# Channel attention in a decoder: the turned scores one head at a time, the turn of the maxima last in its step, two small DVE operations moved, and three unit-matrix products per half

## The chip, the cores and the metric

The kernel runs on one NeuronCore of a Trainium2 chip. The metric is the device time of one execution in microseconds. Five engines work side by side, each through its own instructions in order, and meet at semaphores: PE (TensorE, matmuls), DVE (VectorE), ACT (ScalarE), POOL (GpSimd) and SP (SyncE), which here issues the DMAs.

## The reference

Two decoder layers over 32 x 64 tokens of width 256. The change lies in the second layer's cross attention, which attends between channels. It reads x (normalised) and the context as 16 tiles of 128 tokens; a tile is cut into 32 heads of 4 rows, and a head's 256 columns attend to each other:

```python
def _L1_xattn_ref(qkv, y):
    bs, width, length = qkv.shape
    ch = width // N_HEADS                      # 4 rows of a head
    q = qkv.reshape(bs * N_HEADS, ch, length)
    k = v = y.reshape(bs * N_HEADS, ch, -1)
    scale = 1.0 / math.sqrt(math.sqrt(ch))
    weight = jnp.einsum('bct,bcs->bts', q * scale, k * scale)
    weight = jax.nn.softmax(weight.astype(jnp.float32), axis=-1)
    a = jnp.einsum('bts,bcs->bct', weight, v)
    return a.reshape(bs, -1, length)
```

Ahead of it come attention, cross attention, a feed-forward layer and an attention with linear biases; behind it comes a mixture of 32 experts.

## The kernel before

The stage is software-pipelined by hand. One **slot** t is four heads (one in each group of 32 array rows, `CH_RGS` = 4); a tile has eight slots (`CH_SETS`), a **half** has four (`CH_HALF`), so there are 128 slots and 32 halves. Each slot takes two **steps** n = 2t and 2t+1 (`pair` 0 and 1), of two heads each. In step n, `tensor_step` does for PE, in this order:

1. scores of slot t, two heads, into one of two pairs of PSUM banks (`A`). They wait until DVE has read the bank pair two users before (`s_maxed`).
2. between them, the *turned* scores (keys on the partitions) of an older slot b, 13 steps back, two heads, into three banks (`T`) used in rotation. Both heads wait together for the exponential that frees the later bank (`s_exped`).
3. every eighth step (pair 0, t a multiple of 4; here called the **turn step**): the maxima `m` of the finished half are turned by one transpose into the bank that would be next.
4. the mixing with the values of a slot 16 steps back (L1603). At the first slot of a half it waits for the copy of the last half's outputs (`s_okept`).

DVE (`vector_step`) does one maximum over 128x1024 scores in each step (`top`, L1637), which is what the two score banks are read for. In the turn step it then writes the negated maxima from PSUM to `mT` (L1661), from where SP sends them to the query rows that the turned scores read. `top` of the step after a turn step uses the same bank pair as `top` of the turn step itself, since the transpose has taken the pair between them. ACT takes exp of each turned head (L1623, 128x512) and copies each half's outputs from PSUM (L1632).

A tile's outputs then go round by DRAM, in SP's queue (`sync`), with index n for the tile whose middle is being worked on:

```python
            if 0 <= n - 2 < TILES:
                load_total(n - 2)        # L1490, waits for the stored outputs
            ...
            if 2 * n < CH_HALVES:
                load_max(2 * n)          # L1479, waits for mT of half 2n
            stage(2 * n)                 # L197, a weight chunk of the experts
            ...store_out(2 * n - 2)      # L1483, then queries L1468
                store_inverse(n - 2)     # L1494, waits for invert
            ...
                load_out(n - 2)          # L1500, L1501, waits for that store
```

DVE's `invert(n-2)` (L1644) makes the reciprocal of the sums between L1490 and L1494. POOL's `finish(n-2)` (L1728, L1730) waits for `load_out`, multiplies and adds to x; after it POOL sets the values of the next half (L1723), and SP's `load_v` (L1473) and the next `store_out` (L1483) wait for that. DVE's `measured(n-2)` (L238, statistics of the finished tile, used by the experts' stage much later) waits for `finish(n-2)`.

In the kernel before, DVE does `invert` at t mod 8 = 5 and `measured` at t mod 8 = 3, both behind a `top` of pair 1. The turn steps lie at t mod 8 = 4 (middle of a tile) and t mod 8 = 0 (its end).

Of the kernel before, what the change touches and what calls it, by code (L numbers as in the profile page):

```python
# [15 lines left out]
P = 128  # L16
B, S, D = 32, 64, 256
# [235 lines left out]
def normalise(core, dve, out, tile):  # L253

    return core.nc.vector.tensor_scalar(out, core.x[:, tile, :], core.meanvar[:, tile, 0:1], core.rstd[:, tile, :],  # L255
                                        ALU.subtract, ALU.mult)

# [1137 lines left out]
CH_KEYS_AHEAD = 2  # L1395
CH_AHEAD, CH_SETTLE = 4, 12
# [20 lines left out]
def channel_stage(core, keys, moe, jobs=(), first=0):  # L1417
# [39 lines left out]
    def bank(user):  # L1457
        return A[user % 2]
# [3 lines left out]
    def load_q(sp, tile, parts):  # L1462
        sp.wait_ge(s_lo, tile + 1)
        if tile >= CH_RING:
            sp.wait_ge(s_scoredT, 2 * CH_SETS * (tile - CH_RING + 1))
        for n in parts:
            p, ch = n // CH_CH, n % CH_CH
            sp.dma_start(qp[n:P:32, tile % CH_RING], xs[ch:P:CH_CH, tile % 2, p % 2]).then_inc(q_in[tile % 2], 16)  # L1468
# [6 lines left out]
    def sync(sp):  # L1475
# [33 lines left out]
        for n in range(TILES + 3):  # L1509
# [9 lines left out]
            if CH_KEYS_AHEAD <= n + 2 < TILES:  # L1519
                sp.wait_ge(s_scoredT, 2 * CH_SETS * max(0, n + 2 - CH_RING + 1))  # L1520
                sp.wait_ge(k_in[n % 2], 16 * CH_RGS * (n // 2 + 1))
                keys.load(sp, n + 2, k_in[n % 2])
# [28 lines left out]
    def scores_turned(t, pair, u):  # L1551
        tile, set8 = t // CH_SETS, t % CH_SETS
        for g in (2 * pair, 2 * pair + 1):
            rows = slice(32 * g, 32 * (g + 1))
            last = nc.tensor.matmul(ps[:, T[(t * CH_RGS + g) % len(T)], u * D:(u + 1) * D], kp[rows, tile % CH_RING, set8, u * P:(u + 1) * P],  # L1555
                                    qp[rows, tile % CH_RING, set8, :], start=True, stop=True)
        return last

    def tensor_step(pe, n):
        t, pair = n // 2, n % 2  # L1560
        tile = t // CH_SETS
        b, b_pair = (n - CH_B_LAG) // 2, (n - CH_B_LAG) % 2
        if t < CH_SLOTS:
            if n % (2 * CH_SETS) == 0:
                pe.wait_ge(q_in[tile % 2], 16 * CH_KEYROWS * (tile // 2 + 1))
                pe.wait_ge(k_in[tile % 2], 16 * CH_RGS * (tile // 2 + 1))
            user = (a_first, a_second)[pair](t)
            if user >= 2:
                pe.wait_ge(s_maxed, user - 1)
        if 0 <= b < CH_SLOTS:  # L1570
# [5 lines left out]
            done = b * CH_RGS + 2 * b_pair + 2 - len(T)  # L1576
            if done > 0:
                pe.wait_ge(s_exped, done)
        for u in range(KD):
# [4 lines left out]
            if 0 <= b < CH_SLOTS:  # L1584
                last = scores_turned(b, b_pair, u)
                if u == KD - 1:
                    last.then_inc(s_scoredT, 1)
        if pair == 0 and t % CH_HALF == 0 and 0 < t <= CH_SLOTS:
            half = t // CH_HALF - 1
            user = a_turn(half)  # L1590
            pe.wait_ge(s_maxed, max(user - 1, a_second(t - 1) + 1))
            nc.tensor.transpose(ps[0:32, bank(user), 0:P], m[:, half % 2].rearrange("p g s u -> p (g s u)"), core.ident).then_inc(s_scored, 1)
        c, u = (n - CH_C_LAG) // 2, (n - CH_C_LAG) % 2
        if 0 <= c < CH_SLOTS:
            half, j = c // CH_HALF, c % CH_HALF
            if u == 0:
# [4 lines left out]
                pe.wait_ge(s_exped, CH_RGS * (c + 1))  # L1601
            for g in range(CH_RGS):
# [3 lines left out]
            if u == KD - 1:  # L1606
                last.then_inc(s_mixed, 1)

# [6 lines left out]
    def scalar(act):  # L1615
        for b in range(CH_SLOTS + CH_HALF):
            for g in range(CH_RGS):
                if b < CH_SLOTS:
                    act.wait_ge(s_scoredT, 2 * b + g // 2 + 1)
# [30 lines left out]
    def vector_step(dve, n):  # L1650
# [11 lines left out]
        if pair == 1 and t % CH_SETS == 5 and tile >= 2:  # L1662
            invert(dve, tile - 2)
        if pair == 1 and t % CH_SETS == 3 and tile >= 3:
            measured(dve, tile - 3)
# [942 lines left out]
```

## Time and profile before

| | |
|---|---|
| median of 3 runs | 1909.52 us (1908.63 to 1910.26) |
| the profiled execution | 1909.29 us, span 1907.5 us |
| mean granted TensorE clock | 0.975 |
| PE, DVE, ACT, POOL busy | 89%, 78%, 54%, 38% of the span |
| the channel stage's own steps | 1138.8 to 1502 us |

The span runs from the first to the last instruction; busy shares are averages over six very different stages, so the stretch of the channel stage is looked at by itself. In rows of a timeline the columns are start, duration, engine, line, operation, what it writes and reads, how many were merged, and in brackets how long the engine sat idle before and what ended that.

### The profile page before, as it was taken

The numbers are of one execution on the slowest core, as the hardware profiler recorded it, in microseconds if no ns is written. First come the engines' busy times: TensorE is split into PE (matmuls) and PEld (weight loads), VectorE is DVE, ScalarE is ACT, GpSimd is POOL, SyncE is SP. The second block draws the span as 40 slices with busy tenths as digits, with TensorE's granted clock in tenths as the row PEclk, the third lists the DMA queues.
The fourth block names the chain that finished last, engine by engine and source line by source line (L and its number), as shares of the span: only waits on it lengthen the run. The fifth ranks groups of instructions, "written<-read, shape, count | busy, mean of one in ns | idle before, by whom it ended". The sixth has DMA issues, their size and how long they took to land.

```text
span 1907.5 us, 43444 instructions
## 1 busy us (share of the span) xinstructions
PE 1704.7 (89%) x15840; PEld 1002.3 (53%) x15840; DVE 1488.9 (78%) x2884; ACT 1031.4 (54%) x2056; POOL 720.2 (38%) x965
## 2 busy tenths in 40 slices
PE   5999999789999999979977996777777889999998
PEld 2665666456777777755544541222222356656555
DVE  5776666689989899858887889999999478676654
ACT  2666565345555555534336765888888533323222
POOL 4635321287777677612345452444531000000000
PEclk9999999999999999989989997999999999999999
DMA  9601010000000000000001211333321022222121
GB/s 254 177 24 51 29 42 2 6 18 21 13 13 15 9 9 7 2 9 1 1 1 39 60 36 52 94 90 96 97 74 42 17 79 95 86 65 70 63 84 50
DMA packets 87663, 94.92 MB, mean 50 GB/s; under 512 B 17569, under 2 KB 63265, under 8 KB 87457
## 3 DMA queue, kind: packets, MB, share of 16 engines
q1 hardware_dynamic: 83712, 87.76, 16.1%
q10 hardware_dynamic: 2976, 2.32, 0.5%
q8 instruction: 128, 2.10, 0.5%
q0 software_dynamic: 768, 2.10, 0.4%
q14 instruction: 79, 0.64, 0.1%
HBM read 78.51 MB, written 10.22 MB: 47 GB/s over the span
## 4 chain that ended last, share of the span: by engine, by line
PE 23%; DVE 22%; issue 6%; POOL 3%; ACT 2%; DMA 0%; DVEq 0%; POOLq 0%; ACTq 0%
PE ps L286 18%; DVE arena L1637 14%; POOL arena L1192 2%; PE ps L1904 1%; PE ps L1547 1%; PE ps L1901 1%; DVE arena L2485 1%; DVE arena L2481 0%; DVE arena L1246 0%; DVE arena L255 0%; POOL arena L2058 0%; DVE arena L2416 0%; DVE arena L2414 0%; DVE arena L1997 0%; ACT arena L2357 0%
## 5 line engine op out<-in xcount | busy, mean ns | idle before, releaser
L286 PE MATMUL ps<-arena 128*128 128x512 f16 (+6 forms) x6464 | 1087.7, 323 | 53.1 <-POOL arena L1192 11.1
L286 PEld LDWEIGHTS ps<-arena 128*128 128x128 f16 (+1 forms) x6464 | 600.9, 99 | 438.1 <-issue 36.7
L1623 ACT ACTIVATE arena<-ps 128x512 f32<-128x512 f32 x512 | 278.6, 598 | 73.1 <-PE ps L1555 50.8
L1637 DVE TENSOR_REDUCE arena<-ps 128x4 f32<-128x1024 f32 x256 | 305.6, 1218 | 11.7 <-PE ps L1547 11.4
L1547 PE MATMUL ps<-arena 31*128 31x256 f16 x1024 | 102.5, 277 | 72.9 <-ACT arena L1623 51.7
L1603 PE MATMUL ps<-arena 128*32 128x256 f32 x2048 | 164.9, 394 | 2.8 <-ACT arena L1632 0.6
L2475 DVE TENSOR_TENSOR arena<-ps,arena 128x512 f32<-128x512 f32 x96 | 66.1, 688 | 124.4 <-ACT arena L2367 109.2
L2367 ACT ACTIVATE arena<-ps 128x512 f32<-128x512 f32 x96 | 57.1, 596 | 175.5 <-PE ps L286 175.0
L1547 PEld LDWEIGHTS ps<-arena 31*128 31x128 f16 x1024 | 34.7, 92 | 188.5 <-DVE arena L1637 150.3
L1096 POOL TENSOR_TENSOR arena<-arena 128x512 f32<-128x512 f32 x96 | 98.8, 1043 | 46.1 <-DVE arena L232 44.7
L669 POOL TENSOR_TENSOR arena<-arena 128x256 f32<-128x256 f32 x64 | 39.4, 615 | 194.6 <-DVE arena L635 194.6
L519 ACT ACTIVATE arena<-ps,arena 128x512 f32<-128x512 f32 x64 | 44.0, 688 | 114.9 <-PE ps L286 114.9
L1555 PE MATMUL ps<-arena 32*128 32x256 f16 x1024 | 101.4, 276 | 0.9 <-ACT arena L1623 0.2
L2357 ACT ACTIVATE arena<-arena 128x512 f16<-128x512 f32 x96 | 60.1, 626 | 73.7 <-DVE arena L2481 73.3
L1192 POOL TENSOR_TENSOR arena<-arena 128x512 f16<-128x512 f32 x32 | 50.3, 1575 | 113.8 <-ACT arena L1349 110.5
L208 POOL TENSOR_TENSOR arena<-arena 128x256 f16<-128x256 f32 (+5 forms) x72 | 86.2, 1197 | 5.8
L1110 POOL TENSOR_TENSOR arena<-arena 128x256 f32<-128x256 f32 x80 | 58.2, 728 | 70.2 <-DVE arena L1021 70.1
L955 ACT ACTIVATE arena<-ps 128x512 f16<-128x512 f32 x64 | 38.2, 597 | 83.0 <-PE ps L881 83.0
L206 POOL CAST arena<-arena 128x256 f16<-128x256 f32 (+5 forms) x72 | 45.2, 628 | 95.3 <-DMA arena<-in_L_ffn_gate_up_proj 67.7
L1101 POOL TENSOR_TENSOR arena<-arena 128x512 f32<-128x512 f32 x64 | 67.1, 1049 | 25.3 <-DVE arena L1056 25.2
L1020 DVE TENSOR_TENSOR arena<-ps,arena 128x512 f32<-128x512 f32 x80 | 54.9, 686 | 27.4 <-ACT arena L950 21.7
L588 DVE TENSOR_TENSOR arena<-ps,arena 128x512 f16<-128x512 f32 x64 | 43.9, 686 | 40.7 <-ACT arena L508 40.7
(203 smaller groups left out, 2928.5 us busy)
## 6 DMA issues: line engine op xcount, KB each, us to landing
arena<-moe_cw SPq DMA_DIRECT2D x64, 192.0 KB, 2.8
arena<-moe_cw SPq DMA_DIRECT2D x64, 128.0 KB, 2.8
arena<-in_L_ffn_gate_up_proj SPq DMA_DIRECT2D x16, 384.0 KB, 3.4
ch_out<-arena SPq DMA_DIRECT2D x32, 128.0 KB
arena<-moe_cw SPq DMA_DIRECT2D x64, 64.0 KB, 2.7
ch_keys<-arena SPq DMA_DIRECT2D x48, 64.0 KB, 2.0
arena<-ch_keys SPq DMA_DIRECT2D x64, 48.0 KB
arena<-arena SPq DMA_DIRECT2D x192, 16.0 KB
```

The costliest lines, as they stand in the source:

```text
L208: nc.gpsimd.tensor_tensor(lo, raw, hi, ALU.subtract).then_inc(core.s_split, 1)
L286: last = nc.tensor.matmul(out, a, b, start=start and n == 0, stop=stop and n == len(pairs) - 1, skip_group_check=not group)
L1096: nc.gpsimd.tensor_tensor(a4, a4, spread(rms[:, s % 2, u * CROSS_KVH:(u + 1) * CROSS_KVH], CROSS_HD), ALU.mult).then_inc(scaled.sem, 1)
L1101: nc.gpsimd.tensor_tensor(prob[:, k % 2], e[:, k % 2], spread(inv[:, k % 2, :], CROSS_KEYS), ALU.mult).then_inc(probs.sem, 1)
L1192: nc.gpsimd.tensor_tensor(hT[1][:, k % FFN_MEMBERS], h[:, k // FFN_MEMBERS % 2, k % FFN_MEMBERS], hT[0][:, k % FFN_MEMBERS], ALU.subtract) ...
L1547: last = nc.tensor.matmul(ps[:, bank(user) + n, u * D:(u + 1) * D], qp[rows, tile % CH_RING, set8, u * P:(u + 1) * P], kp[rows, tile % CH_ ...
L1555: last = nc.tensor.matmul(ps[:, T[(t * CH_RGS + g) % len(T)], u * D:(u + 1) * D], kp[rows, tile % CH_RING, set8, u * P:(u + 1) * P], qp[ro ...
L1603: last = nc.tensor.matmul(ps[32 * g:32 * (g + 1), O, 0:D], vz[:, half % 2, u, g, j, :], pT[:, c % 3, g, u, :], start=j == 0 and u == 0, st ...
L1623: nc.scalar.activation(pT[:, b % 3, g], ps[:, T[n % len(T)], :].rearrange("p (u t) -> p u t", u=KD), ACT.Exp, scale=CH_SCALE).then_inc(s_e ...
L1637: nc.vector.tensor_reduce(m[:, half % 2, 2 * half_pair:2 * half_pair + 2, j, :], ps[:, bank(user):bank(user) + 2, :].rearrange("p g (u s) ...
L2357: nc.scalar.activation(hT[0][:, b % 4, :], h[b % MOE_HELD], ACT.Copy).then_inc(s_hi, 1)
L2475: nc.vector.tensor_tensor(h[n % MOE_HELD], ps[:, U[n % 2], :], silu[:, n % 2, :], ALU.mult).then_inc(s_gated, 1)
```

## The change

- The turned scores' two heads are no longer issued together: the first is interleaved with the scores and waits for its own bank, the second follows behind them with a wait of its own. `s_scoredT` counts heads instead of pairs, and the waits on it are scaled.
- In the turn step the transpose of the maxima is issued after the mixing, last.
- `keep_warm` puts three products of the unit matrix with itself (fp32, 128x128 by 128) into the unused columns of the outputs' bank, ahead of the mixing of each half's first slot. By the step numbers this is in the turn step, behind the wait for the copy of the outputs.
- DVE does `invert(n-2)` at t mod 8 = 4 and `measured(n-2)` at the next t mod 8 = 0, each directly behind the write of `mT` in the turn step, instead of three steps later and seven steps later.

```diff
+def keep_warm(nc, out, operand, times):
+    for _ in range(times):
+        nc.tensor.matmul(out, operand, operand, start=True, stop=True, skip_group_check=True)
...
+CH_WARM = 3
...
+        def bank_free(g):
+            done = b * CH_RGS + g + 1 - len(T)
+            if done > 0:
+                pe.wait_ge(s_exped, done)
...
-            done = b * CH_RGS + 2 * b_pair + 2 - len(T)
-            if done > 0:
-                pe.wait_ge(s_exped, done)
+            bank_free(2 * b_pair)
         for u in range(KD):
...
             if 0 <= b < CH_SLOTS:
-                last = scores_turned(b, b_pair, u)
+                last = scores_turned(b, 2 * b_pair, u)
                 if u == KD - 1:
                     last.then_inc(s_scoredT, 1)
-        if pair == 0 and t % CH_HALF == 0 and 0 < t <= CH_SLOTS:
-            (transpose of the maxima)
+        if 0 <= b < CH_SLOTS:
+            bank_free(2 * b_pair + 1)
+            for u in range(KD):
+                last = scores_turned(b, 2 * b_pair + 1, u)
+            last.then_inc(s_scoredT, 1)
...
                 pe.wait_ge(s_exped, CH_RGS * (c + 1))
+                if j == 0:
+                    keep_warm(nc, ps[:, O, D:D + P], core.ident, CH_WARM)
             (mixing)
+        if pair == 0 and t % CH_HALF == 0 and 0 < t <= CH_SLOTS:
+            (transpose of the maxima)
...
-                    act.wait_ge(s_scoredT, 2 * b + g // 2 + 1)
+                    act.wait_ge(s_scoredT, CH_RGS * b + g + 1)
...
             nc.vector.tensor_scalar(mT[:, half % 2], ...).then_inc(s_maxed, 1)
-        if pair == 1 and t % CH_SETS == 5 and tile >= 2:
-            invert(dve, tile - 2)
-        if pair == 1 and t % CH_SETS == 3 and tile >= 3:
-            measured(dve, tile - 3)
+            if t % CH_SETS == CH_HALF and tile >= 2:
+                invert(dve, tile - 2)
+            if t % CH_SETS == 0 and 3 <= tile < TILES:
+                measured(dve, tile - 3)
```

Lines in round brackets stand for code that is moved or kept as it is.

## Rows read from the trace of the kernel before

**Rows 1.** Page: the chain that ended last, share of the span by line.
```profile
PE ps L286 18%; DVE arena L1637 14%; POOL arena L1192 2%; PE ps L1904 1%; PE ps L1547 1%; PE ps L1901 1%; DVE arena L2485 1%; DVE arena L2481 0%; DVE arena L1246 0%; DVE arena L255 0%; POOL arena L2058 0%; DVE arena L2416 0%; DVE arena L2414 0%; DVE arena L1997 0%; ACT arena L2357 0%
```

**Rows 2.** Windows; busy PE, PEld, DVE, ACT, POOL, granted clock, DMA share, GB/s.
```profile
1137.00:1172.00 35.00, 19.09 (x214) 6.41 (x211) 31.52 (x57) 10.53 (x22) 11.06 (x20) 0.61 0.14 39
1197.00:1477.00 280.00, 218.37 (x3483) 68.36 (x3483) 271.02 (x271) 238.84 (x460) 111.58 (x212) 1.00 0.30 81
```

**Rows 3.** Waits, 1157 to 1477: total us, times, longest; the last of SP's queue.
```profile
POOL arena L1728 <- DMA arena<-ch_inverse: 73.1, 13, 12.8
PE ps L1547 <- DMA arena<-arena: 2.0, 4, 1.3
...
SPq L1473 <- POOL arena L1723: 36.9, 12, 3.7
```

**Rows 4.** Timeline of DVE over a half and the next one's start.
```profile
1292.19 0.27 DVE L1661 TENSOR_SCALAR arena<-ps 32x128 f16<-32x128 f32 x1
1292.76 8.51 DVE L1637 TENSOR_REDUCE arena<-ps 128x4 f32<-128x1024 f32 x7 [0.31 <-PE ps L1547]
1301.19 0.42 DVE L238 BATCH_NORM_STATS2 arena<-arena 128x6 f32<-128x256 f32 x1
...
1302.65 0.27 DVE L1661 TENSOR_SCALAR arena<-ps 32x128 f16<-32x128 f32 x1
...
1303.22 3.65 DVE L1637 TENSOR_REDUCE arena<-ps 128x4 f32<-128x1024 f32 x3 [0.31 <-PE ps L1547]
1306.79 0.54 DVE L1644 RECIPROCAL arena<-arena 128x64 f32<-128x64 f32 x1
1307.25 5.69 DVE L1637 TENSOR_REDUCE arena<-ps 128x4 f32<-128x1024 f32 x5
1312.86 0.27 DVE L1661 TENSOR_SCALAR arena<-ps 32x128 f16<-32x128 f32 x1
```

**Rows 5.** Timeline of DVE: the same write of mT ten tiles apart.
```profile
1219.60 0.27 DVE L1661 TENSOR_SCALAR arena<-ps 32x128 f16<-32x128 f32 x1
...
1427.69 0.27 DVE L1661 TENSOR_SCALAR arena<-ps 32x128 f16<-32x128 f32 x1
```

**Rows 6.** Timeline of POOL: the ends of two tiles' finish.
```profile
1295.99 0.73 POOL L1730 TENSOR_TENSOR arena<-arena 128x256 f32<-128x256 f32 x1
...
1316.38 0.73 POOL L1730 TENSOR_TENSOR arena<-arena 128x256 f32<-128x256 f32 x1
1337.18 0.73 POOL L1730 TENSOR_TENSOR arena<-arena 128x256 f32<-128x256 f32 x1
```

**Rows 7.** Timeline of SP's queue from one middle L1479 to the next.
```profile
1305.44 0.56 SPq L1479 DMA_DIRECT2D arena<-arena  x1
1309.46 0.45 SPq L1494 DMA_DIRECT2D ch_inverse<-arena  x1
1311.85 0.63 SPq L1500 DMA_DIRECT2D arena<-ch_out  x1
1317.73 0.39 SPq L1473 DMA_DIRECT2D arena<-in_ctxT  x1
1322.17 0.62 SPq L1490 DMA_DIRECT2D arena<-ch_out  x1
...
1325.84 0.56 SPq L1479 DMA_DIRECT2D arena<-arena  x1
```

**Rows 8.** Timelines of ACT and PE in one turn step, and of PE later.
```profile
1301.06 0.39 ACT L1632 ACTIVATE arena<-ps 128x256 f32<-128x256 f32 x1
...
1301.33 0.28 PE L1592 MATMUL ps<-arena 128*32 128x128 f32 x1
1301.71 0.64 PE L1603 MATMUL ps<-arena 128*32 128x256 f32 x8
...
1518.14 1.05 PE L2272 MATMUL ps<-arena 128*128 128x128 f32 x8
```

**Rows 9.** Timeline of DVE in the low-clock stretch: one maximum and the wait before it.
```profile
1169.69 1.22 DVE L1637 TENSOR_REDUCE arena<-ps 128x4 f32<-128x1024 f32 x1 [0.33 <-PE ps L1547]
```

More of the change, by code:

```diff
@@ L1464, in load_q @@
         if tile >= CH_RING:
-            sp.wait_ge(s_scoredT, 2 * CH_SETS * (tile - CH_RING + 1))
+            sp.wait_ge(s_scoredT, CH_RGS * CH_SETS * (tile - CH_RING + 1))
         for n in parts:
@@ L1519, in sync @@
             if CH_KEYS_AHEAD <= n + 2 < TILES:
-                sp.wait_ge(s_scoredT, 2 * CH_SETS * max(0, n + 2 - CH_RING + 1))
+                sp.wait_ge(s_scoredT, CH_RGS * CH_SETS * max(0, n + 2 - CH_RING + 1))
                 sp.wait_ge(k_in[n % 2], 16 * CH_RGS * (n // 2 + 1))
@@ L1549, in scores, with scores_turned @@
         return last
-    def scores_turned(t, pair, u):
+    def scores_turned(t, g, u):
         tile, set8 = t // CH_SETS, t % CH_SETS
[L1553 to L1557, printed above, removed]
+        rows = slice(32 * g, 32 * (g + 1))
+        return nc.tensor.matmul(ps[:, T[(t * CH_RGS + g) % len(T)], u * D:(u + 1) * D], kp[rows, tile % CH_RING, set8, u * P:(u + 1) * P],
+                                qp[rows, tile % CH_RING, set8, :], start=True, stop=True)
     def tensor_step(pe, n):
@@ L1584, in tensor_step @@
             if 0 <= b < CH_SLOTS:
-                last = scores_turned(b, b_pair, u)
+                last = scores_turned(b, 2 * b_pair, u)
                 if u == KD - 1:
                     last.then_inc(s_scoredT, 1)
-        if pair == 0 and t % CH_HALF == 0 and 0 < t <= CH_SLOTS:
[L1589 to L1592, printed above, removed]
+        if 0 <= b < CH_SLOTS:
[3 more added lines that the diff above has]
+            last.then_inc(s_scoredT, 1)
         c, u = (n - CH_C_LAG) // 2, (n - CH_C_LAG) % 2
@@ L1607, in tensor_step @@
                 last.then_inc(s_mixed, 1)
+        if pair == 0 and t % CH_HALF == 0 and 0 < t <= CH_SLOTS:
+            half = t // CH_HALF - 1
+            user = a_turn(half)
+            pe.wait_ge(s_maxed, max(user - 1, a_second(t - 1) + 1))
+            nc.tensor.transpose(ps[0:32, bank(user), 0:P], m[:, half % 2].rearrange("p g s u -> p (g s u)"), core.ident).then_inc(s_scored, 1)
     def tensor(pe):
```

## The prediction, as recorded before the changed kernel was run

> **What bounds the kernel now.** I read the chain that ended last first [rows 1]. After the matmuls of the other stages, DVE's maximum L1637 is its largest piece, 14% of the span: the channel stage is where the change acts and where DVE sets the pace. The windows give the stage by itself [rows 2]. From 1197 to 1477 us DVE is busy 271.0 of 280 us, ACT 238.8, PE 218.4, and the granted clock is 1.00, the 2.4 GHz level; only up to 1172 us is it lower (0.61). So the stage has a DVE pace of a step, and 9 us of DVE idle to be had there at most.
>
> The timeline of DVE shows the pace inside a half [rows 4]. Two kinds of half alternate. From the mT write at 1292.19 to that at 1302.65 is 10.46 us, from there to 1312.86 is 10.21, so a tile takes 20.67. Seven maxima from 1292.76 take 8.51 us of gapless record, (8.51 - 1.22) / 6 = 1.213 each; five behind the reciprocal, when DVE is behind and its input is ready, take 5.69, (5.69 - 1.22) / 4 = 1.12 each. DVE is thus not quite at its own pace even where it looks full: 0.09 us of each PE-paced step is lost, and the records hide it, since a maximum that overlaps the next one shows no gap. After each turn there is 0.31 us of real idle.
>
> The third thing to see is outside these engines. The waits [rows 3] have POOL waiting for ch_inverse 13 times, 73.1 us, SP for POOL's L1723 12 times, 36.9 us, and PE for an SBUF-to-SBUF DMA 4 times. A tile's outputs go round through SP, the DMAs and POOL, and this round has a period of its own: SP's L1479 comes at 1305.44 and again at 1325.84, 20.40 us later [rows 7], and in this tile it waits for neither PE nor DVE (L1661 was done at 1302.92, the wait before L1473 is POOL's). Ten tiles, from the mT write at 1219.60 to that at 1427.69, average 20.81 us [rows 5], more than the 20.67 of an undisturbed tile: the round already holds PE up now and then. The two periods lie so close that what is saved on one of them alone is mostly lost on the other.
>
> **The moved operations on DVE.** `invert` and `measured` cost 0.46 us (1306.79 to the next maximum at 1307.25) and 0.33 (L238 and the maximum behind it) wherever they stand. Behind mT they lie in the 0.31 us of idle, so placing them there could give back some 0.3 us each. But they also wait. `invert(n-2)` waits for L1490's landing. Its latest place in the old timeline would be mT's end, 1302.92; L1490 is issued 3.67 us before L1479 (1322.17 and 1325.84 [rows 7]), so at 1301.77 here, and the landing is not in a row. Bounds: at once, or by the next issue that needs such a landing, 2.39 us (L1494 at 1309.46 to L1500 at 1311.85). I take 2.3, so 1304.1, a wait of 1.2 us at the old timing.
>
> `measured(n-2)` is the serious one. It moves from 1301.19 to behind the mT write of 1292.19. It waits for `finish`, whose last operation starts at 1295.99 and ends at 1296.72 [rows 6]. Before, that left 4.5 us of slack; in the new place it is 4.26 us *late*. What is queued behind it on DVE is the `top` of the step after the turn; PE waits for that two steps later, and ACT for PE. Added: 1296.72 + 0.05 + 0.33 = 1297.10 instead of 1292.76 for the next maximum, 4.34 us once.
>
> **Why this is not paid only once.** `finish` hangs on the tile's middle mT write by SP's order: L1479 waits for mT, and L1494, L1500, then `finish` stand behind it in the queue. From L1479 to the end of `finish` is 1305.44 to 1317.11 = 11.67 us, and in the next tile 1325.84 to 1337.91 = 12.07 [rows 6, 7]; I take 11.85. With DVE now held up for `finish` at the tile's end, there is a closed loop:
> mT written, to L1479: 0.03; to the end of `finish`: 11.85; to the next maximum: 0.05 + 0.33; from there to the next middle mT write: x.
>
> x follows from the half [rows 4, 8]. Floor by DVE: seven maxima at 1.12 to 1.13, an eighth of 1.22, mT 0.27 less overlap 0.08: 9.33. The chain through PE: the split wait lets the scores start when the maximum two steps back ends, so PE runs ahead of DVE by about a step instead of 0.4 us, and the steps shrink to 1.13. Before, ACT's output copy ended at 1301.45, 8.69 us after the maximum at 1292.76; with seven steps 0.085 shorter and some 0.5 more lead, 7.6. Then 0.26 to the first product, the warm products, the mixing 0.45 (its 0.64 less the tail that a next matmul overlaps), transpose and semaphore 0.32, mT 0.27. A warm product is priced by L2272: eight records of the same shape, two to a product, in 1.05 us, (1.05 - 0.28) / 7 = 0.11 each, so 0.22 a product and 0.66 for three. Sum: 7.6 + 0.26 + 0.66 + 0.45 + 0.32 + 0.27 = 9.56; I take 9.6. If ACT's copy stays at its old 8.69, x is 10.65: both ends are kept.
>
> Period of the loop: 0.03 + 11.85 + 0.38 + 9.6 = 21.86 us, against 20.81 measured: +1.05 per tile. The DVE and PE loop alone would be 9.6 + 9.6 + 0.3 + 0.46, about 19.9, and SP's round 20.4; neither is the largest now. The wait for L1490's landing then hides: L1490 runs ahead of mT by more in the longer period.
>
> **Sum.** Full lag first appears at the turn near 1230: +4.3. From there nine tiles to near 1431 run in the loop: 9 x 1.05 = +9.4. In the last two to three tiles no queries are loaded and the queue is shorter, so DVE and PE go at their own 19.9 against 20.67: -1.5. Behind the stage's last maxima one group of warm products stands in PE's chain: +0.66, less about 0.2 for the split wait. Total +12.7, on the profiled 1909.29: 1922.0. The median of the runs shown is 0.23 above it, so 1922.
>
> **The clock.** The low stretch ends at 1172 and the first warm products come at about 1166; from 1197 to 1477 the clock is full [rows 2], so they have nothing to raise and are counted as 0.66 us each. The Trainium skill (TensorE: Matmul & The Clock Gate, Part 1) says that activity releases the throttle and idleness brings it back. By it the products would be worth something only if PE's idle time grew, which it does here, some 2 us per tile; that is a rival below.
>
> The Trainium skill (DMA: Bandwidth & Descriptors, "Two cost components") puts about 2.0 us on a DMA as fixed cost. From L1500's issue to `finish` the rows have 1315.6 (0.73 before 1316.38) less 1311.85, 3.7 us, for two transfers issued together; by the page's figure the loop would be some 1.7 us shorter and fall below SP's round. The time would then be that of the second rival below. The rows disagree with it here and decide.
>
> **Rivals.**
> *Faster: the waits are satisfied in time.* If `finish` ended before the end-of-tile mT write, DVE would go at 1.13 a step with its extras in the gap, and the stage would gain what SP's round allows at least and 20.67 - 19.9 = 0.77 x 13 tiles = 10 at most: 1899. It needs `finish` 4.3 us earlier than it ends before [rows 6], and nothing in the diff moves it forward. In the loop above it decides from the point where L1479 to the end of `finish` is under 10.8 us, which brings the period back to 20.81. Chance 0.07.
> *No change: SP's round swallows all.* If only that round counts, the time stays at 1906 to 1912. It is against the semaphore count, which makes DVE wait. Chance 0.06.
> *Warm products and late transpose at full price.* x = 10.65, ACT's copy no earlier: +2.1 per tile, 4.3 + 18.9 - 0.5 = +23, 1932. Against it: the exponentials have room. Chance 0.13.
> *The clock falls in the new gaps.* In the low stretch a step took 1.22 + 0.33 = 1.55 us [rows 9] against 1.213. If two to four steps per tile ran so, 0.7 to 1.4 us per tile, 10 to 17 us more: about 1936. Chance 0.04.
> The forecast has 0.70.
>
> **Range.** The loop's bounds are x from 9.33 to 10.65 and L1479 to `finish` from 11.3 (0.4 under the shorter tile) to 12.07: from 4.3 + 9 x 0.23 - 1 = +5 to the +23 above. Of the forecast's own cases I leave the lowest out: 1913 to 1934. The forecast's own range is 1914 to 1930. Changes of under 0.2%, 3.8 us, can hardly be told from none. Faster 0.07, same 0.07 (the second rival and the forecast's lowest end), slower 0.86.
>
> **What the profile after would show.** L238 directly behind L1661 at the tile's end, with idle before it released by POOL L1730, 1.5 to 2 us in each tile from the fourth on; the same mT write 21.9 us apart; maxima 1.13 apart, not 1.213; SP's L1479 in mid-tile waiting for L1661; PE busy 21 us more (96 products of 0.22). I am wrong if DVE never waits for POOL, if the period stays at 20.8 or below, or if the granted clock leaves 1.00 in the stage.

## The result, and the profile after

The changed kernel takes 1930.34 us (median of 4, 1928.29 to 1932.6), the kernel before 1909.89 (median of 4, 1908.63 to 1912.96): a ratio of 1.0104, interval 1.009 to 1.0117. It is slower, as predicted, and by 20.4 us where 12.7 were forecast; 1930.34 lies just above the forecast's own range (1914 to 1930) and inside the stated one (1913 to 1934). The profiled execution took 1929.33 us, its span 1927.5 (before: 1909.29 and 1907.5).

Lines have moved: the maximum is now L1653 (before L1637), the write of mT L1677 (L1661), the reciprocal L1660 (L1644), the turned scores L1561, the mixing L1614 (L1603), the transpose L1623 (L1592), ACT's exponential L1639, its output copy L1648 (L1632), POOL's setting of the values L1739 (L1723), `finish` L1744 and L1746 (L1728, L1730); in SP's queue `load_q` L1475, `load_v` L1480, `load_max` L1486 (L1479), `load_total` L1497 (L1490), `store_inverse` L1501 (L1494), `load_out` L1507 and L1508 (L1500, L1501). The products are L262, `measured` is L238 in both.

The page's chain that ended last, which answers to [rows 1]:

```profile
PE ps L292 18%; DVE arena L1653 5%; PE ps L1614 2%; SPq L1475 2%; DMA arena<-ch_inverse 2%; POOL arena L1198 2%; DMA ch_inverse<-arena 1%; PE ps L1920 1%; PE ps L1554 1%; PE ps L262 1%; PE ps L1917 1%; ACT arena L1639 1%; DVE arena L2501 1%; DVE arena L2497 0%; DMA ch_out<-arena 0%
```

DVE's maximum had 14% of it and has 5%. In its place stand SP's query issues, the store of the inverses, their load, the mixing and the products. The chain now runs through SP, the DMAs to and from DRAM, PE, ACT and DVE. The waits of the stage, 1197 to 1477 us (total, times, longest), and those of SP's queue from 1240 on:

```profile
DVE arena L238 <- POOL arena L1746: 20.3, 12, 2.1
DVE arena L1677 <- PE ps L1623: 15.0, 25, 1.0
PE ps L262 <- ACT arena L1648: 7.1, 18, 0.6
...
SPq L1486 <- DVE arena L1677: 53.0, 22, 6.1
```

The first row is the predicted one: `measured` waits for POOL's last operation in each tile, 1.7 us on the mean. The last is the loop's other joint: SP's `load_max` waits for mT.

The timeline of DVE over the half behind the new wait, and two writes of mT ten tiles apart (answers to [rows 4, 5]):

```profile
1240.78 0.28 DVE L1677 TENSOR_SCALAR arena<-ps 32x128 f16<-32x128 f32 x1 [0.87 <-PE ps L1623]
...
1295.87 0.28 DVE L1677 TENSOR_SCALAR arena<-ps 32x128 f16<-32x128 f32 x1 [0.47 <-PE ps L1623]
1297.36 0.43 DVE L238 BATCH_NORM_STATS2 arena<-arena 128x6 f32<-128x256 f32 x1 [1.21 <-POOL arena L1746]
1297.70 9.13 DVE L1653 TENSOR_REDUCE arena<-ps 128x4 f32<-128x1024 f32 x8
1307.30 0.28 DVE L1677 TENSOR_SCALAR arena<-ps 32x128 f16<-32x128 f32 x1 [0.47 <-PE ps L1623]
1307.51 0.53 DVE L1660 RECIPROCAL arena<-arena 128x64 f32<-128x64 f32 x1
...
1330.14 0.28 DVE L1677 TENSOR_SCALAR arena<-ps 32x128 f16<-32x128 f32 x1 [0.77 <-PE ps L1623]
...
1465.88 0.28 DVE L1677 TENSOR_SCALAR arena<-ps 32x128 f16<-32x128 f32 x1 [0.87 <-PE ps L1623]
```

L238 stands right behind L1677 with idle released by POOL. Eight maxima take 9.13 us, (9.13 - 1.22) / 7 = 1.13 each: DVE works at its own pace again, and waits 0.47 us for the transpose at the half's end. The period is (1465.88 - 1240.78) / 10 = 22.51 us, against 20.81 [rows 5].

The other stations of the loop: POOL (answers to [rows 6]),

```profile
1296.48 0.73 POOL L1746 TENSOR_TENSOR arena<-arena 128x256 f32<-128x256 f32 x1
...
1318.71 0.73 POOL L1746 TENSOR_TENSOR arena<-arena 128x256 f32<-128x256 f32 x1
```

SP's queue (answers to [rows 7]),

```profile
1307.61 0.56 SPq L1486 DMA_DIRECT2D arena<-arena  x1
...
1311.63 0.44 SPq L1501 DMA_DIRECT2D ch_inverse<-arena  x1
1314.23 0.63 SPq L1507 DMA_DIRECT2D arena<-ch_out  x1
```

and ACT and PE in the turn step between (answers to [rows 8]):

```profile
1304.92 0.39 ACT L1648 ACTIVATE arena<-ps 128x256 f32<-128x256 f32 x1
...
1305.57 0.91 PE L262 MATMUL ps<-arena 128*128 128x128 f32 x6 [0.55 <-ACT arena L1648]
1306.41 0.64 PE L1614 MATMUL ps<-arena 128*32 128x256 f32 x8
1306.98 0.28 PE L1623 MATMUL ps<-arena 128*32 128x128 f32 x1
```

From `load_max` at 1307.61 to the end of `finish` at 1319.44 is 11.83 us; POOL's end at 1297.21 to L238 is 0.15, L238 to the maximum 0.34, and from the maximum at 1297.70 to mT's end at 1307.58 is 9.88.

One thing is in the trace that the forecast did not have. The windows (columns as in [rows 2]):

```profile
1197.00:1477.00 280.00, 234.00 (x3355) 83.64 (x3349) 242.93 (x250) 216.51 (x423) 110.35 (x204) 0.95 0.28 79
1320.00:1321.50 1.50, 0.31 (x8) 0.13 (x8) 1.50 (x3) 0.00 (x0) 1.43 (x3) 1.00 0.65 232
1321.50:1325.00 3.50, 3.50 (x40) 0.90 (x40) 3.27 (x4) 2.38 (x5) 3.29 (x4) 0.51 0.49 126
```

The stage's granted clock is 0.95, not 1.00. Behind the wait for `finish` PE is idle, then it is granted 0.51, the 1.2 GHz level, for 3.5 us. PE's timeline shows the edge:

```profile
1318.83 0.64 PE L1614 MATMUL ps<-arena 128*32 128x256 f32 x8
1321.19 0.28 PE L1554 MATMUL ps<-arena 31*128 31x256 f16 x2 [1.73 <-DVE arena L1653]
...
1321.53 1.08 PE L1614 MATMUL ps<-arena 128*32 128x256 f32 x8
```

The same eight mixing matmuls take 0.64 us ahead of the gap and 1.08 behind it. Such a stretch begins 6 times between 1240 and 1477, and never there in the kernel before. In the tile with this one the half behind the wait took 10.5 us, from the maximum at 1319.92 to mT's end at 1330.42, instead of 9.88. The six such halves took 10.49 to 10.69 us, 0.74 more than 9.88 on the mean; the four others of the ten tiles took 9.88 each. Every tile has an idle time of PE behind the wait: 1.47 to 1.98 us in the six, 0.89 to 1.53 in the four.

Where the 20 us are: the first write of mT was at 1152.9 before and is at 1148.5, the last at 1478.5 and 1496.4, so the stage itself is 22.3 us longer; behind the last one lie 429.0 and 431.1 us, +2.1; and the stage starts 4.5 earlier, which is no gain of the change (that start lies between 1148.5 and 1155.5 in the profiles of this study, whose kernels have the same code ahead of it).

### The profile page after: what moved, and what is told of

The parts are those of the page before. It is cut to its first block, busy times and chain, and to the rows that moved or that the text cites. A ratio compares the mean times of both kernels' runs of the same rounds, so it can differ in the third digit from the quotient of the medians.

```text
span 1927.5 us, 43766 instructions
## 1 busy us (share of the span) xinstructions
PE 1738.4 (90%) x15971; PEld 1029.6 (53%) x16032; DVE 1482.3 (77%) x2884; ACT 1026.2 (53%) x2056; POOL 720.5 (37%) x965
## 3 DMA queue, kind: packets, MB, share of 16 engines
q8 instruction: 129, 2.11, 0.5%
## 4 chain that ended last, share of the span: by engine, by line
PE 26%; DVE 13%; issue 6%; POOL 4%; DMA 3%; SPq 3%; ACT 2%; DVEq 0%; POOLq 0%; ACTq 0%
PE ps L292 18%; DVE arena L1653 5%; PE ps L1614 2%; SPq L1475 2%; DMA arena<-ch_inverse 2%; POOL arena L1198 2%; DMA ch_inverse<-arena 1%; PE ps L1920 1%; PE ps L1554 1%; PE ps L262 1%; PE ps L1917 1%; ACT arena L1639 1%; DVE arena L2501 1%; DVE arena L2497 0%; DMA ch_out<-arena 0%
## 5 line engine op out<-in xcount | busy, mean ns | idle before, releaser
L1639 ACT ACTIVATE arena<-ps 128x512 f32<-128x512 f32 x512 | 272.4, 599 | 101.4 <-PE ps L1561 98.0
L1653 DVE TENSOR_REDUCE arena<-ps 128x4 f32<-128x1024 f32 x256 | 292.6, 1206 | 2.5 <-PE ps L1554 1.8
L1614 PE MATMUL ps<-arena 128*32 128x256 f32 x2048 | 171.3, 408 | 0.1
L2383 ACT ACTIVATE arena<-ps 128x512 f32<-128x512 f32 x96 | 57.1, 596 | 175.7 <-PE ps L292 175.3
L1554 PE MATMUL ps<-arena 31*128 31x256 f16 x1024 | 105.2, 287 | 48.9 <-DVE arena L1653 46.9
L1561 PE MATMUL ps<-arena 32*128 32x256 f16 x1024 | 117.9, 284 | 0.0
L1554 PEld LDWEIGHTS ps<-arena 31*128 31x128 f16 x1024 | 29.5, 93 | 158.6 <-DVE arena L1653 123.2
```

The source lines that it names most:

```text
L1554: last = nc.tensor.matmul(ps[:, bank(user) + n, u * D:(u + 1) * D], qp[rows, tile % CH_RING, set8, u * P:(u + 1) * P], kp[rows, tile % CH_ ...
L1561: return nc.tensor.matmul(ps[:, T[(t * CH_RGS + g) % len(T)], u * D:(u + 1) * D], kp[rows, tile % CH_RING, set8, u * P:(u + 1) * P], qp[ro ...
L1614: last = nc.tensor.matmul(ps[32 * g:32 * (g + 1), O, 0:D], vz[:, half % 2, u, g, j, :], pT[:, c % 3, g, u, :], start=j == 0 and u == 0, st ...
L1639: nc.scalar.activation(pT[:, b % 3, g], ps[:, T[n % len(T)], :].rearrange("p (u t) -> p u t", u=KD), ACT.Exp, scale=CH_SCALE).then_inc(s_e ...
L1653: nc.vector.tensor_reduce(m[:, half % 2, 2 * half_pair:2 * half_pair + 2, j, :], ps[:, bank(user):bank(user) + 2, :].rearrange("p g (u s) ...
```

## The experiments

Theory A: the moved `measured` closes a loop (DVE waits for POOL's `finish`, which hangs by SP's order on the mT that the same DVE wrote half a tile earlier), and this loop is the loss. Theory B: the loss is PE's part, the products and the late transpose, and the wait only shows it. Theory C: part of the loss is the clock, which falls in the gaps that the wait leaves on PE. A fourth, E, is about what the other parts are worth: SP's round through DRAM has its own period near 20.4 us and takes what they save. The letters are those of the recorded expectations, which add D, F, G and H where they stand.

All readings in one table. The period is over ten tiles, between the starts of two rows of DVE's timeline, L1677 (or L1661), like those above; "low" counts the stretches from 1240 to 1477 us in which the eight mixing matmuls took over 0.9 us, and the clock is that window's granted one.

| kernel | median us | ratio [interval] | profiled us | mT at | period | clock | low |
|---|---|---|---|---|---|---|---|
| before | 1909.89 | | 1909.29 | 1240.26, 1448.35 | 20.81 | 1.00 | 0 |
| changed | 1930.34 | 1.0104 [1.009, 1.0117] | 1929.33 | 1240.78, 1465.88 | 22.51 | 0.96 | 6 |
| e1, moves undone | 1911.77 | 1.001 [0.9999, 1.002] | 1910.29 | 1240.51, 1446.26 | 20.58 | 1.00 | 0 |
| e2, moves alone | 1920.39 | 1.0054 [1.0035, 1.0073] | 1920.69 | 1241.97, 1458.10 | 21.61 | 0.99 | 2 |
| e3, no products | 1919.69 | 1.005 [1.0034, 1.0067] | 1919.66 | 1241.88, 1459.85 | 21.80 | 0.94 | 8 |
| e4, PE's part, no products | 1910.82 | 1.000 [0.9983, 1.0017] | 1910.9 | 1240.83, 1448.19 | 20.74 | 0.99 | 2 |
| e5, `measured` alone | 1932.41 | 1.0109 [1.0095, 1.0124] | 1928.93 | 1244.42, 1465.59 | 22.12 | 0.97 | 4 |
| e6, `invert` alone | 1911.9 | 1.0001 [0.999, 1.0011] | 1916.41 | 1243.65, 1454.51 | 21.09 | 1.00 | 0 |
| e7, e4 + shorter round | 1907.82 | 0.9968 [0.9953, 0.9983] | 1911.42 | 1241.21, 1444.96 | 20.38 | 0.96 | 5 |
| e8, before + shorter round | 1910.08 | 0.999 [0.9979, 1.0001] | 1906.57 | 1238.33, 1444.95 | 20.66 | 1.00 | 0 |
| e9, e1 + shorter round | 1908.75 | 0.9987 [0.9978, 0.9996] | 1910.41 | 1243.92, 1447.21 | 20.33 | 1.00 | 0 |
| e10, e9, products elsewhere | 1923.74 | 1.007 [1.0056, 1.0083] | 1922.66 | 1242.94, 1458.40 | 21.55 | 0.99 | 2 |
| e11, changed, `finish` earlier | 1911.28 | 1.0001 [0.9991, 1.0011] | 1916.06 | 1244.19, 1452.58 | 20.84 | 1.00 | 0 |
| e12, e9, one product | 1902.37 | 0.9964 [0.995, 0.9978] | 1899.86 | 1238.04, 1437.96 | 19.99 | 1.00 | 0 |

Each ratio is against runs of the kernel before beside it; their medians were 1909.18 to 1911.56. Period, clock and low stretches are of the one profiled execution, which can lie off the median: it is the slowest of its runs in e6 and e7 and the fastest in e5, e10 and e12. The mean clock over the whole kernel is known for every run; on the mean of the runs it is 0.968, 0.970 and 0.967 in e3, e4 and e7, which have no products, 0.974 in e1, e9 and e12, which have them in the turn step and not the loop, and 0.974 to 0.976 in the kernel before.

**e1, the DVE moves undone** in the changed kernel (e2 is the opposite edit, on the kernel before):

```diff
-            if t % CH_SETS == CH_HALF and tile >= 2:
-                invert(dve, tile - 2)
-            if t % CH_SETS == 0 and 3 <= tile < TILES:
-                measured(dve, tile - 3)
+        if pair == 1 and t % CH_SETS == 5 and tile >= 2:
+            invert(dve, tile - 2)
+        if pair == 1 and t % CH_SETS == 3 and tile >= 3:
+            measured(dve, tile - 3)
```

> The changed kernel with DVE's two moved operations back in their old places (invert at t mod 8 = 5, measured at t mod 8 = 3, pair 1); the split wait, the late transpose and the three products stay. Theory A (the move of measured closes a loop mT, SP's queue, finish on POOL, DVE, which gives the period): DVE's waits for POOL go, the tile period falls from 22.5 us to SP's round of about 20.4 to 20.8, and the early gain of 4.5 us (turn steps up to 1200 us) stays in part: 1903 to 1909 us. Theory B (the products and the late transpose on PE give the time, the waits only sit beside them): 1925 to 1930, about as the changed kernel. Theory C (part of the +20 is the clock falling in PE's gaps while DVE waits): the granted clock stays 1.00 from 1200 to 1480 us.

1911.77 us: 18.6 of the 20.4 us are gone with all of PE's part still in. Its window, 1240 to 1477:

```profile
1240.00:1477.00 237.00, 210.06 (x3114) 81.42 (x3106) 224.57 (x231) 195.64 (x391) 92.57 (x176) 1.00 0.29 80
```

The clock is 1.00 with the products in and the long waits out. This refutes theory B as the main cause, and it agrees with C's condition (clock 1.00). A's time was a little low: what PE's part was to give did not come (the period is only 0.23 below that of the kernel before).

**e2, the moves alone**, on the kernel before.

> The kernel before with DVE's two operations moved as in the change, nothing else of it. Theory A: the loop closes here too, with the old half of about 9.9 us between the resumed maxima and the next mT write: period 0.03 + 11.8 + 0.4 + 9.9 = 22.1 or more, without the gain of the early turn steps, so 1927 to 1935 us. Theory B: 1905 to 1911, since nothing of PE's work changes. Theory C: low-clock stretches of 3.4 us appear here as well.

1920.39 us, +10.4, so only about half of the loss, below what A expected. DVE's timeline:

```profile
1296.38 0.27 DVE L1661 TENSOR_SCALAR arena<-ps 32x128 f16<-32x128 f32 x1
1298.91 0.43 DVE L238 BATCH_NORM_STATS2 arena<-arena 128x6 f32<-128x256 f32 x1 [2.25 <-POOL arena L1730]
1299.25 9.12 DVE L1637 TENSOR_REDUCE arena<-ps 128x4 f32<-128x1024 f32 x8
1308.29 0.27 DVE L1661 TENSOR_SCALAR arena<-ps 32x128 f16<-32x128 f32 x1
```

Here mT comes without any wait behind eight maxima at DVE's pace: x = 1308.56 - 1299.25 = 9.31. With the prediction's other terms the loop is 0.03 + 11.85 + 0.38 + 9.31 = 21.57; 21.61 was measured. The loop's formula holds, and the prediction's lower bound of x, 9.33, is what the old PE order has. That the two agree within 0.04 is in part luck: measured link by link it is 0.03 + 11.69 + 0.49 + 9.41 = 21.62, where 9.41 is 9.31 and what the two low stretches add.

**e3, no products** (`CH_WARM = 0` in the changed kernel), and **e4**, the same with the moves undone too, so PE's split wait and late transpose alone:

> The changed kernel with no unit-matrix products (CH_WARM = 0), all else as changed. Theory A with the products at full price in the half (0.66 us between ACT's copy and the next mT write): period 0.66 shorter per tile, 9 to 12 tiles, 6 to 8 us: 1922 to 1925 us. Theory B: the turn step is freed of the products, 2 x 0.66 per tile or 20 us less: 1910. Theory C: without the products PE is idle longer, more low-clock stretches than the seven between 1200 and 1480 us, and no gain: 1928 to 1935.

> The changed kernel with DVE's operations back and no products: only the split wait and the late transpose are left. Theory A: as e1, since SP's round of 20.4 to 20.8 us is the limit there and the products are hidden under it: within 2 us of e1, 1903 to 1909. Theory B: 0.66 us per half less than e1 or more, 15 to 20 us below it. Theory C: clock 1.00 or a little lower; if the products were what kept it, low stretches appear here and not in e1.

e3's window and its main wait:

```profile
1240.00:1477.00 237.00, 192.12 (x2839) 59.88 (x2834) 213.61 (x221) 190.89 (x375) 89.25 (x169) 0.94 0.28 78
```

```profile
DVE arena L238 <- POOL arena L1746: 21.1, 10, 2.8
```

Without products 1919.69, lower than the 1922 to 1925 expected; with them 1930.34. So the products cost 10.7 us *inside the loop*, where every tile has them between ACT's copy and mT. With the moves undone, e4 and e1, they cost 1.0 us, no more than the noise: there another round sets the pace. And without them the clock falls more often, 8 stretches instead of 6, so the 10.7 is what is left after whatever they give. The moves cost 1919.69 - 1910.82 = 8.9 us without products and 18.6 with them. So half of the 20.4 us needs both: the loop that the move closes, and the products in it. The time of e3 also speaks against C's expectation for it (no gain); its count of low stretches is as C has it, and low stretches appear in e4 and not in e1. e4 equals before: the late transpose and the split wait alone bring nothing that shows.

**e5 and e6, one move each** on the kernel before; e5's edit:

```diff
+            if t % CH_SETS == 0 and 3 <= tile < TILES:
+                measured(dve, tile - 3)
-        if pair == 1 and t % CH_SETS == 3 and tile >= 3:
-            measured(dve, tile - 3)
```

> The kernel before with measured alone moved behind mT at t mod 8 = 0; invert stays at t mod 8 = 5. Theory A (measured closes the loop): as the kernel with both moved (1920.4, period 21.6 us), since invert's wait is covered there: 1918 to 1923 us. Rival D (invert's wait for the landing of the sums makes the cost): as before, 1908 to 1911.

> The kernel before with invert alone moved behind mT at t mod 8 = 4; measured stays at t mod 8 = 3. Theory A: DVE waits for the landing of the sums, which come 2.3 us after L1490, so each tile's phase against SP's round shifts by about 1.2 us once, then the period stays that of SP's round: 1908 to 1912. Rival D: 1918 to 1923.

`invert` alone costs nothing, 1911.9 (no change). (e6 is the like edit for `invert`.) `measured` alone costs 21.5 us, twice as much as both moves together, which I had not expected. SP's queue in e5:

```profile
1312.60 0.56 SPq L1479 DMA_DIRECT2D arena<-arena  x1
...
1317.02 0.35 SPq L1494 DMA_DIRECT2D ch_inverse<-arena  x1
1317.47 1.67 SPq L1468 DMA_DIRECT2D arena<-arena  x3
1319.25 0.63 SPq L1500 DMA_DIRECT2D arena<-ch_out  x1
```

`store_inverse` comes 4.42 us behind `load_max`, against 4.02 [rows 7]: with `invert` left at t mod 8 = 5 it runs three maxima behind mT (1316.45, mT at 1312.31), so the reciprocal is a link of the loop. In e2 `invert` is done by then. From `load_max` to the end of `finish` is 12.06 us on the mean of ten tiles, 11.69 in e2: 0.37 of the 0.51 by which the periods differ, and four low stretches instead of two make up the rest. That is read from one trace of each and not tested by an edit, and it gives 5 of the 11 us between the medians; the other part is not shown. The seat of the loss is `measured`; `invert` early is a help once that loop exists.

**e7, e8, e9: SP's round shortened.** `load_total`, which waits for stored outputs to land, is moved behind `load_max`, which then no longer stands behind that wait:

```diff
-            if 0 <= n - 2 < TILES:
-                load_total(n - 2)
...
             if 2 * n < CH_HALVES:
                 load_max(2 * n)
+            if 0 <= n - 2 < TILES:
+                load_total(n - 2)
```

e7 is e4 with it, e8 the kernel before with it, e9 is e1 with it (so e7 with the three products).

> The changed kernel without products, with DVE's operations in their old places, and in SP's queue load_total (with its wait for the stored outputs) placed behind the five queries and load_max of the tile's middle instead of ahead of them. Theory E (in the kernel before and without the moves, SP's round of DRAM trips, 20.4 to 20.8 us a tile, sets the period and PE waits for the mT transfer that stands in it): load_max no longer waits for the landing, the PE and DVE pace of about 19.9 to 20.0 us shows: 0.6 to 0.8 us less per tile over 12 tiles, 1900 to 1904 us. Rival F (the stage is DVE's 20.7 anyway): 1910, as e4.

> The kernel before with only that reordering of SP's queue. Theory E: its own PE pace is 20.67 against the 20.81 measured, so only 0.14 x 12 = 1.7 us can come: 1907 to 1909. Rival F: the same as before within 1 us.

> As the run with the shortened round (DVE's operations in their old places, load_total behind load_max), but with the change's three products in the turn step. There the clock fell for 3.4 us about every second tile without them, and an undisturbed tile took 19.98 us, a disturbed one about 1 us more. Theory G (the products keep the clock up and cost less than they bring once nothing else binds): no low-clock stretch between 1240 and 1477 us, every tile 20.3 to 20.5 us (the products' 0.8 us in one half show in part): 0 to 2 us faster or slower than without, 1904 to 1910. Theory H (products only cost): 2 x 0.8 us a tile or some of it, 5 to 10 us slower than without them: 1912 or more.

e8 is no faster beyond doubt: 1910.08, with a period of 20.66 that is the undisturbed pace of a tile in the kernel before (20.67). So PE and DVE bound that kernel together as much as the round does. e4 has the quicker step but the old round, and is no faster either. With both, e7, the period falls to 20.38 and the kernel is 0.3% faster: theory E holds. The traces show the wait that went. In e4 PE stands idle ahead of L1554 six times between 1240 and 1477, 6.1 us in all, for what the profile calls issue; in e7 never. The longest in e4, rows of SP and PE:

```profile
1344.03 0.62 SPq L1497 DMA_DIRECT2D arena<-ch_out  x1
1348.02 0.56 SPq L1486 DMA_DIRECT2D arena<-arena  x1
1349.82 0.28 PE L1554 MATMUL ps<-arena 31*128 31x256 f16 x2 [2.87 <-issue]
```

mT was written at 1342.73, but `load_max` comes behind `load_total` and the queries, and PE goes on 1.8 us after it. (That this idle time is the wait for `load_max` is inferred from the order, the profile does not name it.)

e7 missed the 1900 to 1904 of theory E by some 4 us. DVE's timeline and the window of a low stretch show what held it:

```profile
1301.75 1.22 DVE L1653 TENSOR_REDUCE arena<-ps 128x4 f32<-128x1024 f32 x1 [0.30 <-PE ps L1554]
1303.29 1.23 DVE L1653 TENSOR_REDUCE arena<-ps 128x4 f32<-128x1024 f32 x1 [0.32 <-PE ps L1554]
1304.86 1.23 DVE L1653 TENSOR_REDUCE arena<-ps 128x4 f32<-128x1024 f32 x1 [0.34 <-PE ps L1554]
```

```profile
1301.50:1305.20 3.70, 3.70 (x48) 0.88 (x40) 2.79 (x3) 2.48 (x5) 0.00 (x0) 0.54 0.36 77
```

There a step takes 1.55 us (the 1.55 of [rows 9]), about 1 us lost per stretch, 5 stretches. e9's three products remove them all, but a tile without stretches takes 20.30 to 20.33 instead of 19.98: 1908.75 against e7's 1907.82, no better.

**e10, the products off the turn step**: in e9 the three are moved from ahead of the mixing to the end of the next step, into the free half of the transpose's bank pair.

```diff
-                if j == 0:
-                    keep_warm(nc, ps[:, O, D:D + P], core.ident, CH_WARM)
...
+        if pair == 1 and t % CH_HALF == 0 and 0 < t < CH_SLOTS:
+            keep_warm(nc, ps[:, bank(a_turn(t // CH_HALF - 1)) + 1, 0:P], core.ident, CH_WARM)
```

> As the last one, but the three products stand at the end of the step behind the turn step, into the free half of the bank pair that the transpose took, where PE has about 1 us of lead over DVE, and not between ACT's copy and the transpose. Theory G: the clock stays up and the tile takes its undisturbed 20.0 us: 0.6 to 0.8 us a tile less than the kernel before over 14 tiles, 1899 to 1903 us. Theory H: no difference to the run without products, 1907, or slower.

A miss, 1923.74 where I had expected 1899 to 1903. DVE's timeline behind the turn, and PE's:

```profile
1298.04 1.23 DVE L1653 TENSOR_REDUCE arena<-ps 128x4 f32<-128x1024 f32 x1 [0.30 <-PE ps L1554]
1299.81 6.88 DVE L1653 TENSOR_REDUCE arena<-ps 128x4 f32<-128x1024 f32 x6 [0.55 <-PE ps L1554]
```

```profile
1298.51 0.94 PE L262 MATMUL ps<-arena 128*128 128x128 f32 x6
```

Behind the turn DVE has caught up with PE and waits for its scores; the products lie right ahead of them. The second maximum waits another 0.55 us. The products' place has no idle of PE that they could fill.

**e11, the changed kernel with `finish` earlier.** Nothing on DVE or PE is touched. In SP's queue `store_inverse` goes right behind `load_max`, and `load_out` ahead of the last queries:

```diff
             if 2 * n < CH_HALVES:
                 load_max(2 * n)
+            if 0 <= n - 2 < TILES:
+                store_inverse(n - 2)
...
                 load_q(sp, n + 2, range(5, 9))
+            if 0 <= n - 2 < TILES:
+                load_out(n - 2)
```

(both are taken out of their old places)

> The changed kernel, all of it, with SP's queue cut short between load_max and finish: store_inverse directly behind load_max, load_out behind the next four queries. From L1486's issue to the end of finish that takes away about 2.0 us of 11.8. Theory A (the loop mT, SP, finish, DVE gives the period of 22.5 us): the period falls by as much, to 20.4 to 20.8, and DVE's waits for POOL shrink: 1908 to 1913 us. Theory B (PE's products and late transpose give the period by themselves): 1926 to 1930.

1911.28 us: 19 of the 20.4 us come back by the order of SP's queue alone. Its SP queue and POOL, and the wait:

```profile
1307.24 0.55 SPq L1486 DMA_DIRECT2D arena<-arena  x1
1307.84 0.45 SPq L1501 DMA_DIRECT2D ch_inverse<-arena  x1
...
1311.79 0.62 SPq L1507 DMA_DIRECT2D arena<-ch_out  x1
```

```profile
1316.65 0.73 POOL L1746 TENSOR_TENSOR arena<-arena 128x256 f32<-128x256 f32 x1
```

```profile
DVE arena L238 <- POOL arena L1746: 4.1, 6, 1.5
```

From `load_max` to the end of `finish` is 1317.38 - 1307.24 = 10.14 us instead of 11.83, and the period is 20.84. This is the case that shows theory A: the loop is what costs, since a shorter link in it, which touches nothing else on DVE or PE, gives the time back. The low stretches went with it (0 in the window), though all three products are still in.

**e12, one product instead of three** in e9.

```diff
-CH_WARM = 3
+CH_WARM = 1
```

> The run with the shortened round and products in the turn step, but one product instead of three. With three the tile took 20.30 us and the clock stayed full from 1240 us; with none an undisturbed tile took 19.98 and five low-clock stretches stood between 1240 and 1477 us. Theory G (the products hold the clock, and each costs PE's turn step about 0.25 us of which part shows): either one product holds the clock too and the tile takes about 20.1, 1904 to 1907 us, or it doesn't, low stretches appear as without products and the time is theirs, 1906 to 1910. Theory H (the low stretches have nothing to do with the products): their number is that of three products, about one.

1902.37 us, 0.9964 [0.995, 0.9978], below both kernels and below the 1904 to 1907 expected. Its window, and PE's turn step:

```profile
1240.00:1477.00 237.00, 204.62 (x3065) 71.79 (x3057) 226.57 (x258) 201.97 (x402) 91.62 (x176) 1.00 0.30 80
```

```profile
1296.52 0.46 PE L262 MATMUL ps<-arena 128*128 128x128 f32 x2 [0.54 <-ACT arena L1648]
1296.91 0.64 PE L1614 MATMUL ps<-arena 128*32 128x256 f32 x8
1297.48 0.28 PE L1623 MATMUL ps<-arena 128*32 128x128 f32 x1
```

The clock is 1.00 with no low stretch, and the period is 19.99, the undisturbed tile of e7. One product from 1296.52 to the mixing at 1296.91 is 0.39 us, three are 0.84 (1305.57 to 1306.41): 0.225 for each further one, and 0.17 once beside the first. Against three products (e9, 0.9987 [0.9978, 0.9996]) one is the faster. Against none (e7, 0.9968 [0.9953, 0.9983]) the runs do not tell: the ratios are alike, and the periods of 19.99 and 20.38 come from e12's fastest and e7's slowest run. That the products hold the clock is seen in all runs; that one product saves time over none is not shown.

## Why the prediction was right, and where its sizes were off

**The mechanism: right, and shown.** DVE waits in each tile for POOL, behind the mT write of the tile's end; the wait closes a loop. e1 (wait out, loss out), e2 and e5 (wait in, loss in) and e11 (wait in, link shortened, loss out) leave no other main cause. The point from which the loop decides, `load_max` to the end of `finish` under 10.8 us, agrees with e11: 10.14 and a period of 20.84. But one of the three signs by which the forecast was to be wrong did come: the granted clock left 1.00 in the stage. And 1930.34 is nearer to the 1932 of the rival "warm products and late transpose at full price" than to 1922. That rival is not what happened: it had ACT's copy no earlier and x = 10.65, and the copy came at 7.6 us and x is 9.88 wherever the clock stays up.

**The link through SP and POOL: right.** 11.85 us was taken; 11.83 in the tile shown, 11.67 on the mean of ten. The step from POOL's end to the next maximum was 0.15 + 0.34 instead of 0.38, 0.1 short. The rows decided rightly here against the shorter DMA cost that the recorded text weighed, though its 3.7 us are no measure of one transfer: the second load is issued 0.67 us after the first (L1501 at 1312.52), and each moves 128 KB.

**x, from there to mT: mis-sized.** 9.6 was taken and 9.88 measured. The copy on ACT ended 7.6 us after the resumed maximum (1305.31 - 1297.70), exactly as taken. The products took 0.84 us instead of 0.66, since the price came from a row of eight records in series (0.22 each, e12 confirms 0.225) and left out the 0.17 once beside the first. The mixing ahead of the transpose took 0.57 instead of 0.45. That is the 0.3. e2 and e3 put a size on what the late transpose and the products do to the loop: the period is 21.61 with neither, 21.80 with the transpose late, 22.51 with both. All three hold low stretches; in the tiles without one x is 9.31, 9.32 and 9.88. So the late transpose (with the split wait) costs the loop nothing, and three products cost it 0.56 us a tile of their 0.84.

**The clock: what the forecast left at 0.04 happened beside it.** The recorded text named "the clock falls in the new gaps" as a rival; it is no rival but comes on top. The period by the measured links without it is about 0.03 + 11.67 + 0.49 + 9.88 = 22.07. Six of the ten tiles lost 0.74 us on the mean, 0.44 a tile, which gives 22.51, as measured. So of the excess of 0.65 over the forecast's 21.86, two thirds are the clock, and one third is the turn step's 0.28 and 0.11 behind `finish`, less 0.18 for the shorter link through SP. The price in the rival, 0.7 to 1.4 us per tile, holds for a tile with a stretch at its lower end (0.61 to 0.81), but only six tiles in ten had one.

**The clock again: "they have nothing to raise".** This is wrong for the quicker step. With split wait and late transpose and no products, the clock falls 2, 5 and 8 times (e4, e7, e3), although no gap in e7 comes from the loop. The kernel before, with its slower step, keeps 1.00. There is something to raise, and one product raises it (e12). At the stage's start the granted clock reached 1.00 near 1164.5 in the changed kernel and near 1172 in the one before; but e1, with the products, has 1167.5 and e3, e4 and e7, without them, 1168 to 1172, so no run shows that they raise it there. The Trainium skill (TensorE: Matmul & The Clock Gate, Part 1) has it that idleness brings the throttle back; the changed kernel agrees, where each of the six stretches comes behind 1.47 to 1.98 us of idle on PE. Why the quicker step in e7 is more exposed than the slower one before, which leaves PE idle for longer (busy 16.13 us of 20.60 in a tile, against 16.56 of 19.99 in a tile of e7 without a stretch), no run here settles. The traces give a hint: the idle time of e7 comes in a longer piece. Its longest is 0.78 us, once in each tile behind the turn step, and all five stretches begin right behind it; the kernel before has at most 0.44 there, and e12 and e9, with products, hardly anything over 0.6. It is no more than a hint, since single gaps of 1.26 us before and 1.48 in e1 passed without a fall.

**The sum.** Forecast +4.3 for the first lag, +9.4 for nine tiles, -1.5 at the end, +0.5 behind: 12.7. Measured: +5.0 up to the write of mT at 1240.78, +17.0 over the ten tiles from there (1.70 each instead of 1.05, and one tile more in the loop), +0.3 at the end, where the gain of 1.5 did not come, +2.1 behind the stage. The 5.0 is not one lag of 4.3: DVE waits for `finish` already near 1207, 2.11 us, and again near 1230, 1.95, each time with a low stretch behind it. The stage's earlier start takes 4.5 off. Of the +2.1 I can name only the product group and a clock of 0.95 instead of 0.98 between 1477 and 1580 us; it was not tested.

**What the other parts give.** That DVE and PE alone would run at "about 19.9" was right: e12 has 19.99. That SP's round near 20.4 would swallow it was right as well (e1 and e4 no faster than before), and moving one wait in its queue gave it free (e7, e12). PE's busy time rose by 33.7 us, not 21: the page has 1738.4 against 1704.7. Low-clock stretches count as busy, but they are the smaller part of it: e1, with none between 1240 and 1477, has 1735.3, and e4, without products, 1715.5.

**Still open:** why the clock falls in the quicker pattern; what else makes e5 slower than e2; the 7 us between starts of the stage in kernels with the same code ahead of it, which is why differences of that size between the times of single profiles say nothing here; the +2.1 behind the stage; and whether one product in the changed kernel as it stands would have cost less, which was not run.

## What to carry to other kernels

Before an operation that waits for another engine is moved forward in an in-order queue, follow what it waits for back to its start. If that hangs on an earlier output of the same engine, the wait is not paid once but closes a loop: add up its links, and compare the period with those of the other loops. A filler instruction is nearly free only outside the loop that sets the pace (three products: 1 us there, 10.7 inside), so try one before three (e12, e9); and where two rounds lie within 2%, neither edit alone moves the time (e4, e8), but both do (e7, e12).

## What the runs showed of the hardware that was not expected

In this stage PE's granted clock drops to the 1.2 GHz level for some 3.5 us at a time (0.51 to 0.54 in the windows), in the case shown behind 1.7 us of idle, and comes back. A mixing group of 0.64 us takes 1.08 in it. One fp32 product of 128x128 by 128x128 every ten microseconds, 0.39 us of PE, kept the clock at 1.00 in a pattern in which it fell five times in 237 us without it (one trace of each; over all runs the kernel's mean clock is 0.974 against 0.967); three kept it no better and cost 0.3 us more per tile. In the changed kernel, whose waits were longer, three did not hold it.
